# Exact attention scores computed in two halves of TensorE's rows, with a new order of the work and a root by logarithm and exponential

## The reference, cut to what matters

```python
# block 1: gated cross attention, 16 heads of 8 features
xn = layernorm(x); q = xn @ Wq + bq; k = ctx @ Wk + bk; v = ctx @ Wv + bv
x1 = x + tanh(g_xattn) * (softmax(q k^T / sqrt(8)) v @ Wo + bo)
# block 2: gated transformer block with four experts
x2 = layernorm(x1); h = rms(x2) * n1
q = rms_head(h @ wq.T) * qn; k = rms_head(h @ wk.T) * kn; v = h @ wv.T
x2 = x2 + causal_attention(q, k, v) @ wo.T         # first 32 features stay
xf = rms(x2) * n2; gates = top-2 softmax of xf @ gate_w.T
moe = gates . (gelu expert, silu expert, four-layer gelu expert, three-layer gelu expert)
out = x1 + tanh(g_ffn) * (x2 + moe)                # first 32 features of moe are 0
```

## Time and profile before

| what | us |
|---|---|
| median of the runs (3) | 1075.44 |
| lowest and highest | 1074.19, 1075.52 |
| the profiled execution's own time | 1072.52 |
| its span | 1070.7 |
| granted TensorE clock | 0.987 of full speed |

### The profile page before, as it was taken

One profiled execution on the slowest core, in us unless ns is written; L12 is line 12 of the kernel. 1 busy time (PEld: TensorE's weight loads), 2 busy tenths in 40 slices (PEclk: granted clock), 3 DMA queues, 4 the chain that ended last, 5 costly groups with the idle time before them and its releaser, 6 DMA issues.

```text
span 1070.7 us, 26205 instructions
## 1 busy us (share of the span) xinstructions
PE 1004.9 (94%) x8649; PEld 626.3 (58%) x8649; DVE 789.2 (74%) x2172; ACT 736.1 (69%) x1334; POOL 337.8 (32%) x463
## 2 busy tenths in 40 slices
PE   6678799999999999999999999999999999999898
PEld 5445456566665656666565666656566665655565
DVE  8667777877787787778778777877877777774723
ACT  6466677676777767677776767777676777767453
POOL 5615134051513405151240515124051512404130
PEclk9989899999999999999999999999999999999999
DMA  7433432233343233434323343432234343221200
GB/s 233 134 106 130 136 112 93 90 102 127 115 142 111 90 92 103 127 115 140 109 92 92 106 127 115 136 109 93 90 111 127 115 135 109 82 67 62 69 1 20
DMA packets 77317, 114.28 MB, mean 107 GB/s; under 512 B 7776, under 2 KB 40160, under 8 KB 77152
## 3 DMA queue, kind: packets, MB, share of 16 engines
q1 hardware_dynamic: 76800, 111.53, 33.0%
q10 hardware_dynamic: 480, 2.26, 0.6%
HBM read 58.97 MB, written 53.74 MB: 105 GB/s over the span
## 4 chain that ended last, share of the span: by engine, by line
PE 64%; DVE 15%; ACT 11%; issue 7%; DMA 1%; SPq 1%; POOL 0%; DVEq 0%; ACTq 0%
PE ps_pv L1362 9%; PE ps_w L1388 9%; PE ps_s2a L1341 7%; PE ps_s2b L1341 5%; PE ps_s2a L1400 5%; PE ps_s2b L1407 4%; PE ps_t L1224 4%; ACT probs L951 4%; PE ps_w L1407 3%; DVE mpadB L1091 3%; PE ps_w L1273 3%; DVE mpadA L1091 3%; PE ps_t L1375 2%; PE ps_w L1224 2%; PE ps_w L1305 2%
## 5 line engine op out<-in xcount | busy, mean ns | idle before, releaser
L951 ACT ACTIVATE probs<-ps_s2a 120x512 f32<-120x512 f32 (+1 forms) x256 | 153.4, 599 | 73.1 <-PE ps_s2a L1341 64.7
L1091 DVE TENSOR_REDUCE mpadB<-ps_w 128x4 f32<-128x512 f32 x240 | 148.8, 684 | 24.9 <-PE ps_w L1305 24.9
L1091 DVE TENSOR_REDUCE mpadA<-ps_w 128x4 f32<-128x480 f32 x224 | 131.5, 651 | 38.0 <-PE ps_w L1305 38.0
L951 ACT ACTIVATE probs<-ps_s2b 120x512 f32<-120x512 f32 (+1 forms) x256 | 153.6, 600 | 0.0
L818 POOL TENSOR_SCALAR_AFFINE_SELECT probs<-probs 128x1024 f32<-128x1024 f32 x128 | 139.8, 1092 | 0.0
L1388 PE MATMUL ps_w<-W,hid 128*128 128x96 f32 x976 | 122.5, 279 | 1.0 <-DVE split_k L985 0.9
L1388 PEld LDWEIGHTS ps_w<-W,hid 128*128 128x128 f32 x976 | 114.9, 193 | 10.4 <-issue 4.9
L786 POOL TENSOR_TENSOR rB<-vrB,neg_half 128x4 f32<-128x4 f32 x16 | 16.1, 1007 | 207.2 <-DVE veB L978 207.2
L1341 PE MATMUL ps_s2a<-qdA,kstA 128*120 128x512 f32 x128 | 68.7, 537 | 7.0 <-ACT probs L951 3.1
L1400 PE MATMUL ps_s2a<-hid,W 128*128 128x512 f32 x152 | 74.4, 604 | 0.0
L1120 DVE SCALAR_TENSOR_TENSOR ym<-ps_w,gates,ym 128x96 f32<-128x96 f32 x184 | 45.7, 311 | 38.5 <-PE ps_w L1388 38.5
(11 more groups left out here) (279 smaller groups left out, 2166.7 us busy)
## 6 DMA issues: line engine op xcount, KB each, us to landing
scratch_Aq<-split_q SPq DMA_DIRECT2D x48, 256.0 KB, 2.4
qdA<-scratch_Aq SPq DMA_DIRECT2D x64, 192.0 KB
scratch_Bq<-split_q SPq DMA_DIRECT2D x48, 256.0 KB, 2.4
scratch_Bk<-split_k SPq DMA_DIRECT2D x48, 256.0 KB, 2.9
qdB<-scratch_Bq SPq DMA_DIRECT2D x64, 192.0 KB
kstB<-scratch_Bk SPq DMA_DIRECT2D x64, 192.0 KB
scratch_Ak<-split_k SPq DMA_DIRECT2D x48, 240.0 KB, 2.3
kstA<-scratch_Ak SPq DMA_DIRECT2D x64, 180.0 KB
```

Of the source, the lines that this page charges most:

```text
L951: nc.scalar.activation(probs[0:k, slot_of(part, *index), :], bank[0:k, :], ACT.Exp, scale=SCALE if part == "A" else 1.0).then_inc(done, 1)
L1091: nc.vector.tensor_reduce(pair[:, :, c, b % 2] if halves else mneg[p][:, :, c, b], bank[:, 0:HT * k].rearrange("p (h k) -> p h k", h=HT), ...
```

## The change

The parts of the diff are these. Exact scores: the rows of the four heads of a chunk are spread over two halves of the array, heads 0 and 1 in rows 0 to 47 with their maximum in row 48, heads 2 and 3 in rows 64 to 111 with row 112. `qd` is then half as large. An exact pair is now four matmuls of 49 rows and 256 columns: two for the upper half (chunk c, then c+1) into `s2a`, then two for the lower half into `s2b`. A bank thus holds two heads of two chunks, so `pv` picks its queries by `c // 2 * 2 + j // 2`, and in the cross attention it waits for both banks of the pair. The loads of stacks and maxima go to the new rows; their count is the same. The setup clears less, because `qd` is smaller.

Order: `pv` can be issued in two halves (`early_values`, `late_values`), and `down` of experts 0 and 3 in two halves (`head`, `rest`). These halves and other uses are placed anew between the exact pairs, and two of the three estimates of A that stood among the exact pairs move. The step that fills the pipeline last (t = 2) uses the new order too; the first three and the last three steps keep theirs.

Root: `hr = exp(-0.5 * ln(hs/8 + eps))` by two ACT operations in place of Sqrt on ACT and a reciprocal on DVE.

The diff, cut to its core:

```diff
@@ -89,9 +89,19 @@
     return [(part, "s1", (b, c), rings[c]) for c in range(NT)]
-def values(part, b):
-    return [(part, "pv", (b, c), "pv" if b % 2 and c == NT - 1 else None) for c in range(NT)]
+def values(part, b, first=0, last=NT):
+    return [(part, "pv", (b, c), "pv" if b % 2 and c == NT - 1 else None) for c in range(first, last)]
+def early_values(part, b):
+    return values(part, b, 0, PACK)
+def late_values(part, b):
+    return values(part, b, PACK, NT)
...
@@ -104,42 +114,54 @@
     return [(part, "fill", (name, c), ring)]
-def down(e):
-    return fill("M", "down", e, "w")
+HEADED = (0, 3)
+def head(e):
+    return one("M", "head", e, None)
+def rest(e, ring="w"):
+    return fill("M", "down", e, ring)
+def down(e, ring="w"):
...
+    return (head(e) if e in HEADED else []) + rest(e, ring)
 def self_attention():
-    return (one("N", "load", 0, None) + one("N", "ctx", 0, None) + exact("D", 0, 0) + one("B", "hT") + down(1) + exact("D", 0, 2)
-            + one("B", "qk", 0) + one("B", "qk", 1) + one("B", "qk", 2) + one("B", "qk", 3)
-            + exact("D", 1, 0) + estimate("A", 0) + exact("D", 1, 2)
-            + one("B", "squares", 0, None) + values("D", 0)
-            + exact("D", 2, 0) + estimate("A", 1) + exact("D", 2, 2)
-            + values("D", 1) + one("B", "sums", 0, None) + down(0)
-            + exact("D", 3, 0) + one("D", "oT", 0, "t") + estimate("A", 2) + exact("D", 3, 2)
-            + one("A", "base", 0, None) + values("D", 2) + one("D", "nT", 0, "t") + one("B", "root", 0, None))
+    return (one("N", "load", 0, None) + one("N", "ctx", 0, None) + exact("D", 0, 0) + one("B", "hT") + down(1)
+            + exact("D", 0, 2) + one("B", "qk", 0) + one("B", "qk", 1) + early_values("D", 0)
+            + exact("D", 1, 0) + one("B", "qk", 2) + one("B", "qk", 3) + late_values("D", 0)
+            + exact("D", 1, 2) + one("B", "squares", 0, None) + estimate("A", 0) + early_values("D", 1)
+            + exact("D", 2, 0) + head(0) + late_values("D", 1)
+            + exact("D", 2, 2) + rest(0) + one("D", "oT", 0, "t") + one("B", "sums", 0, None) + estimate("A", 1)
+            + exact("D", 3, 0) + early_values("D", 2) + one("D", "nT", 0, "t") + late_values("D", 2)
+            + exact("D", 3, 2) + one("A", "base", 0, None) + one("B", "root", 0, None))
 def second_experts():
-    return (fill("M", "e2_l2", 0) + one("D", "wo", 0, "t") + one("B", "scale", 0, None) + fill("M", "e2_l2", 1)
-            + estimate("A", 3) + values("D", 3) + fill("M", "e3_up", 0) + one("D", "oT", 1, "t") + fill("M", "e3_up", 1)
-            + one("N", "stats", 0, None)
-            + one("D", "nT", 1, "t") + one("A", "mT") + fill("M", "e2_l3", 0) + one("N", "norm", 0, None) + one("D", "wo", 1, "t")
-            + one("D", "out", 0, None) + one("B", "qT") + one("B", "kT") + one("D", "squares", 0, None)
-            + fill("M", "e2_l3", 1, "w"))
+    return (one("D", "wo", 0, "t") + early_values("D", 3) + fill("M", "e2_l2", 0) + one("B", "scale", 0, None) + estimate("A", 2)
+            + late_values("D", 3) + fill("M", "e2_l2", 1) + estimate("A", 3) + fill("M", "e3_up", 0) + one("D", "oT", 1, "t")
+            + fill("M", "e3_up", 1) + one("N", "stats", 0, None) + one("A", "mT") + fill("M", "e2_l3", 0) + one("D", "nT", 1, "t")
+            + one("B", "qT") + one("B", "kT") + one("N", "norm", 0, None) + one("D", "wo", 1, "t")
+            + one("D", "out", 0, None) + one("D", "squares", 0, None) + fill("M", "e2_l3", 1, "w"))
 def cross_attention():
-    return (exact("A", 0, 0) + one("B", "v") + down(2) + exact("A", 0, 2) + one("N", "xT")
-            + exact("A", 1, 0) + estimate("B", 0) + exact("A", 1, 2)
-            + one("D", "norm", 0, None) + one("B", "init", 0, None) + one("B", "copy", 0, None) + values("A", 0)
-            + exact("A", 2, 0) + estimate("B", 1) + exact("A", 2, 2)
-            + values("A", 1) + down(3) + one("M", "store", 0, None) + one("D", "xfT")
-            + exact("A", 3, 0) + one("A", "oT", 0, "t") + estimate("B", 2) + exact("A", 3, 2)
-            + values("A", 2) + one("D", "logits") + one("A", "nT", 0, "t"))
+    return (exact("A", 0, 0) + one("B", "v") + down(2) + exact("A", 0, 2) + one("N", "xT") + estimate("B", 0)
+            + exact("A", 1, 0) + values("A", 0) + one("D", "norm", 0, None) + one("B", "init", 0, None) + one("B", "copy", 0, None)
+            + exact("A", 1, 2) + head(3) + early_values("A", 1)
+            + exact("A", 2, 0) + rest(3) + one("M", "store", 0, None) + estimate("B", 1)
+            + exact("A", 2, 2) + late_values("A", 1) + one("D", "xfT")
+            + exact("A", 3, 0) + one("A", "oT", 0, "t") + early_values("A", 2) + estimate("B", 2)
+            + exact("A", 3, 2) + one("D", "logits") + late_values("A", 2) + one("A", "nT", 0, "t"))
...
-        qd = {p: sb("qd" + p, [P, HT, NT, TOK], F32R) for p in "AB"}
+        qd = {p: sb("qd" + p, [P, HT // 2, NT, TOK], F32R) for p in "AB"}
         kst = {p: sb("kst" + p, [P, NT, G * keys[p]], F32R) for p in "AB"}
...
         GROUP_STACKS, GROUP_M, USE_STORED = 16 * 2 * HT, 16, 16 * SPLIT
-        M_ROW = HD * SPLIT * HT
+        HALF_ROWS, M_ROW = P // 2, HD * SPLIT * HT // 2
...
-            return qd[p][M_ROW:M_ROW + 1, :, :, :].rearrange("p j c (b q) -> p (j c b) q", b=G).bitcast(F32)
+            return qd[p][M_ROW:P:HALF_ROWS, :, :, :].rearrange("p j c (b q) -> p (j c b) q", b=G).bitcast(F32)
+        def rows_of_head(j):
+            first = j // 2 * HALF_ROWS + j % 2
+            return slice(first, first + M_ROW, 2)
         def half_of_maxima(p, half, b):
...
                     for j in range(HT):
-                        at = slice(j, M_ROW, HT)
+                        at = rows_of_head(j)
                         of = scratch[to + o].rearrange("(c j r) t -> j r c t", j=HT, r=rows)[j]
-                        to_tile = qd[to][at, j, :, :] if o == "q" else kst[to][at, :, :]
+                        to_tile = qd[to][at, j % 2, :, :] if o == "q" else kst[to][at, :, :]
                         sp.dma_start(to_tile.bitcast(F32), of[:, :, 0:to_tile.shape[-1]]).then_inc(stacks_loaded[to], 16)
             def load_half(st, part, work):
...
                         act.wait_ge(hs_ready, g + 1)
-                        nc.scalar.activation(hr[:], hs[:], ACT.Sqrt, bias=rms_eps[:, 0:1], scale=1.0 / HD).then_inc(root_ready, 1)
+                        nc.scalar.activation(hl[:], hs[:], ACT.Ln, bias=rms_eps[:, 0:1], scale=1.0 / HD).then_inc(log_ready, 1)
+                        act.wait_ge(log_ready, g + 1)
+                        nc.scalar.activation(hr[:], hl[:], ACT.Exp, scale=-0.5).then_inc(root_ready, 1)
                     elif (part, work) == ("B", "qT"):
                         if st.first("B"):
...
                         dve.wait_ge(root_ready, g + 1)
-                        nc.vector.reciprocal(hr[:], hr[:]).then_inc(hr_ready, 1)
-                        dve.wait_ge(hr_ready, g + 1)
                         nc.vector.tensor_tensor(
                             qk[:].rearrange("p b (h d) -> p (b h) d", d=HD), qk[:].rearrange("p b (h d) -> p (b h) d", d=HD),
                             hr[:].rearrange("p (n a) -> p n a", a=1).to_broadcast([P, 2 * H * G, HD]), ALU.mult)\
...
                             pe.wait_ge(half_loaded[p][1], (g + 1) * 2 * GROUP_M)
-                        for bk, v in st.drains([], key):
-                            pe.wait_ge(drained[bk], v)
-                        o = bank[0:k, :].rearrange("p (h q) -> p h q", h=HT)
-                        mm(o, kst[p][:, c, b * k:(b + 1) * k], qd[p][:, :, c, b * P:(b + 1) * P],
-                           start=True, stop=True).then_inc(done, 1)
+                        if c % 2:
+                            continue
+                        tiles = [(part, "s2", (b, c + half)) for half in range(2)]
+                        for half in range(2):
+                            for bk, v in st.drains([], tiles[half]):
+                                pe.wait_ge(drained[bk], v)
+                            for cc in range(2):
+                                rows = slice(half * HALF_ROWS, half * HALF_ROWS + M_ROW + 1)
+                                o = psum[st.bank[tiles[half]]][0:k, cc * 2 * P:(cc + 1) * 2 * P].rearrange("p (h q) -> p h q", h=2)
+                                ins = mm(o, kst[p][rows, c + cc, b * k:(b + 1) * k], qd[p][rows, :, c + cc, b * P:(b + 1) * P],
+                                         start=True, stop=True)
+                                if cc:
+                                    ins.then_inc(filled[st.bank[tiles[half]]], 1)
                     elif work == "pv":
                         b, c = index
                         p = OP[part]
                         k = keys[p]
                         last = (part, "pv", (b | 1, NT - 1))
-                        sources = [(part, "s2", index)] if part == "A" else []
```

(31 more changed lines are left out.)

28 lines of the change are left out of this document (12 added, 16 removed).

## The result

| | median us | lowest and highest | runs | ratio to before, 95% interval |
|---|---|---|---|---|
| before, same chip | 1074.82 | 1073.59 to 1075.52 | 4 | |
| after | 1217.08 | 1205.11 to 1237.9 | 4 | 1.129 [1.120, 1.138] |

The change makes the kernel 142 us slower. The forecast said slower, 1139, with 1164 as its upper end; the truth lies 53 us above that end. The profiled execution took 1220.31 us.

A forecast was written before the change was run, and what follows sets the result against it. TensorE, busy 94% of the span, was taken to bound the kernel, with a quarter of the chain others' work. +4.7 us a trip, 56 in 12 trips, plus 7 and 1 elsewhere gave about 1139 us, range 1072 to 1164.

The forecast's parts named there:

- TensorE's own time and small waits together: Per trip: changes of shape 3.8 us less 1.4 gained on exact pairs, +2.4; waits that go, -2.7.
- before A's fourth estimate: TensorE waits 2.1 us a trip: root with two table loads, then scale and the third estimate's maxima on DVE.
- before B's first: TensorE waits 1.4 us (bounds 0 and 2.2) for DVE to finish draining `down` 2 before B's first estimate.
- before B's second: B's second estimate directly follows the rest of `down` 3 and waits 1.1 us for DVE's drain.
- before A's second: A's second estimate, behind `down` 0 with only transposes between, waits 0.7 us, 0.4 more than before.
- The waits that come: New TensorE waits before four estimates in a loop trip: 2.1, 1.4, 1.1 and 0.4 us more.
- Exact pairs: Four half-array matmuls in three steps, 0.54 us a pair; 16 pairs take 8.6 us, a gain of 1.4 a trip.
- The second rival: Cheap shape changes, two-step pairs; half the gain becomes longer waits: 65.4 us a trip, 1115; chance 0.22 shared with fewer loads.
- The root: Ln then Exp on ACT bring two table loads, 3.4 us, ahead of scale and A's fourth estimate.
- The rival with one load: Ln and Exp need one table load: -1.3 us a trip, 1122 us; chance 0.22 shared with no load or cheap halves.
- DMA and SP at nothing: DMA counts and bytes unchanged, SP 2 us or more in hand: cost nothing; late stacks would add their delay per trip.
- The sum: Trip 62.5 to 67.2 us, 56 us in 12 trips; steps 2 and 15 add 7, other steps 1: 1136.5 us profiled.

The follow-up runs named there:

- e_order: Kernel before with the new order and split uses alone, exact matmuls whole and Sqrt kept: 1161.9 us, ratio 1.082.
- e_order_busy: Kernel before with the new order alone, whole matmuls and Sqrt, plus 6, 8 and 5 dummy matmuls in its three long loop waits: 1146.2 us.
- e_busy: Kernel after with dummy matmuls that nobody reads in the loop's three long waits before estimates: 1181.5 us, ratio 1.097.
- e_mended2: Kernel after with Sqrt, halves of 64 rows, and several uses moved away from what they waited for: 1135.8 us, ratio 1.056.

## Why the prediction was right and where it failed

Step by step, by full-clock trips:

| term | predicted | measured |
|---|---|---|
| a pair | 0.54 | 0.44 |
| TensorE's own time and small waits together | +2.4 - 2.7 = -0.3 | -0.3 (5.65 less the 5.9 of the four waits) |
| before A's fourth estimate | 2.1 | 2.15 |
| before B's first | 1.4 | 2.1 |
| before B's second | 1.1 | 1.25 |
| before A's second | 0.7 (0.4 more than before) | 0.74 (0.4 more) |
| trip | 67.2 | 68.2 |

- *The waits that come* were right in place, releaser and size, all four; B's first was 0.7 dearer than the term, near its upper bound. Of the 5.65 us this is nearly all, and e_order has it without the other two parts.
- *Exact pairs* were 0.10 cheaper each: two steps, not three. I had taken three because of the order in which the program issues them, and the trace shows the lower half passing by. The Trainium skill, "TensorE: Matmul & The Clock Gate", Part 3, which I followed, says that matmuls start in program order; for two halves of the array the rows of 385.05 say otherwise, and the measurement decides. The gain didn't reach the trip: 16 pairs at 0.10 less are 1.6 us, yet own time and small waits together came out at the -0.3 of the sum, and e_order, without the halves, has the same trip within 0.1 us. So a right figure for the pair would have made the forecast of the trip worse, and it is partly luck that this line fits. The second rival had said that half of such a gain would be lost in longer waits; here all of it was. That DVE's strict order is what took it is likely, but no run shows it.
- *The root* has the two loads that I took from the earlier trace rows. The rival with one load is out. The Trainium skill, "ScalarE: Activation LUTs", Table sets, has ln and exp in one set; here each had its own load of 1.28 us, and whether another choice of table would save one was not tried.
- *DMA and SP at nothing* held in the trip, where no wait of PE ends with a transfer. It failed in the filling: there TensorE waits for the stacks until 29.6 us where it waited until 26.5, and the first long fall of the clock begins in that wait.
- *The sum* is the step that failed, by two terms that it put at nothing or nearly so: the clock, and the filling with the end. It was made with durations of a profiled execution at a clock of 0.987, and I took this clock for granted in the kernel after. Of the 84 us between its 1136.5 and the profiled 1220.3, 12 are the trips at full clock (1.0 each), 37 the clock in the loop, and 35 the filling and the end, which grew by 27.6 + 15.4 where I had 8 in all; there the time at half clock rose by 75 and by 27 us. Each part of the change lengthens the filling when it is alone, the order by 11.2 us, the halves by 13.7 and the root by 7.9, and the halves alone lengthen the end by 10.8. The rows to ask were there: the kernel before has falls at 50 and 118 us, each inside a wait of TensorE (4.4 us up to 51.7, 5.0 us up to 120.6), and at 67 and 90 us, behind waits of 2.5 and 2.2 us. I added waits of 2 us without asking what they do to the clock.

With the order alone and the waits filled (e_order_busy, 1146 us) the forecast of 1139 is 7 us short; with the clock free to fall the same waits cost 1162, and with halves 1211. The direction and the mechanism of the waits in the loop were right; the clock was missing from it, and the size, 64 us, was less than half of the measured 142.

Open: by what the chip decides when it lowers the clock. The same waits of 2.1 us stand in every trip of after, and half of the trips have no fall; outside the loop some falls, such as those at 1109 and 1161 us in after, begin near waits of only 0.7 us. Open too is how much of the filling's 27.6 us is the clock and how much waits: its first fall in after lasts 44 us, but e_busy, with the same code there, has one of 17 us and a filling as long. What a change from or to the shape of a half costs by itself was not isolated.

## What to carry to other kernels

Read the granted clock as a term of its own: a wait of two us that comes once or twice a trip was paid here at its length and then again, by 37 us in the loop, in what ran behind it. Price the filling and the end of a pipeline too: they cost 43 of the 148 us here, and a forecast made from one trip of the loop does not see them. Before an order is changed to take away small waits, list for every use that needs several banks at once what fills and drains the last of them; four such waits made this change. Where a wait can't be taken away, matmuls that nobody reads, put inside it and ending before it does, are a cheap test of whether the clock is part of the loss, and here sometimes a gain.

## What the runs showed of the hardware

- Two matmuls in the two halves of the array's rows start 0.01 us apart, also where the program doesn't alternate them, and a pair of four takes 0.44 us. Their weight loads, in the same trip:

```profile
385.05 0.18 PEld L1370 LDWEIGHTS ps_s2a<-qdB,kstB 49*128 49x128 f32 x1
385.06 0.18 PEld L1370 LDWEIGHTS ps_s2b<-qdB,kstB 49*128 49x128 f32 x1
```

- The clock fell behind waits of 2.1 us in the middle of a loop that is otherwise full (after), and in e_mended2 behind waits of 0.86 us, but not in every trip: the first five trips of after, 177 to 519 us, have the waits and no fall.
- Rows that hold zeros, and change no result and not the length of a trip at full clock, shortened the falls behind B's first estimate from mostly 17.1 to mostly 3.4 us.
- Two activation functions that follow each other, Ln and Exp, had a table load of 1.28 us each, although the function before Ln was an Exp.
